# Context values computed inside an earlier attention, with two smaller edits, in a two-layer decoder kernel

## The reference, cut to what matters

```python
# layer 0, cross attention
q = _qdq(x) @ _qdq(wq).T + bq
k, v = jnp.split(cond @ wkv.T + bkv, 2, axis=-1)
attn = softmax(einsum('bnhd,bmhd->bhnm', q, k) * scale)
out = _qdq(einsum('bhnm,bmhd->bnhd', attn, v)) @ _qdq(wp).T + bp
# layer 1, cross attention
q = _rms_norm(draft_hidden @ Wq.T, q_norm_w)
kv_in = concatenate([context_hidden, draft_hidden], axis=1)
k = _rms_norm(kv_in @ Wk.T, k_norm_w)      # then rope on q and k
v = kv_in @ Wv.T                           # no norm, no rope
```

## Time and profile before

| what | value |
|---|---|
| time, median of 3 runs | 2729.94 us (2729.03 to 2731.29) |
| time of the profiled execution | 2728.3 us |
| its span | 2726.6 us, 48715 instructions |
| mean granted clock of PE | 0.951 of 2.4 GHz |
| PE, matmuls | 2479.4 us busy (91%) |
| PE, weight loads | 2033.7 us (75%) |
| DVE | 1704.5 us (63%) |
| ACT | 1154.6 us (42%) |
| POOL | 934.5 us (34%) |
| HBM | 123 GB/s over the span |

### The profile page before, as it was taken

The page is one execution under the profiler, slowest core; times in us unless marked ns, Lnnn a source line. Parts: engine busy times, 40 slices in busy tenths (PEclk is TensorE's granted clock), DMA queues, the critical chain, the costliest instruction groups (busy, mean ns, idle before and its releaser), DMA issues. The chain is left out here.

```text
span 2726.6 us, 48715 instructions
## 1 busy us (share of the span) xinstructions
PE 2479.4 (91%) x14967; PEld 2033.7 (75%) x14968; DVE 1704.5 (63%) x3211; ACT 1154.6 (42%) x2389; POOL 934.5 (34%) x943
## 2 busy tenths in 40 slices
PE   7999788879899999799997998997999998999998
PEld 7888666658688887588875886665777787888887
DVE  4536847769777666676675566866555535666564
ACT  2103256623343334455553233757655522444443
POOL 4203201134333234423333212753333312355554
PEclk9999989989899989899998988998999989999999
DMA  5544122125622055477774432444222131666664
GB/s 191 154 140 114 28 93 77 46 91 168 179 68 65 15 166 182 147 220 223 195 223 105 131 68 96 151 125 126 73 70 72 55 129 63 182 163 159 147 163 73
DMA packets 304547, 336.59 MB, mean 123 GB/s; under 512 B 149231, under 2 KB 220063, under 8 KB 302578
## 3 DMA queue, kind: packets, MB, share of 16 engines
q1 hardware_dynamic: 233170, 256.24, 30.1%
q0 software_dynamic: 20640, 51.74, 9.7%
q10 hardware_dynamic: 50560, 26.34, 3.3%
HBM read 235.70 MB, written 98.56 MB: 123 GB/s over the span
## 5 line engine op out<-in xcount | busy, mean ns | idle before, releaser
L898 PE MATMUL e_psum<-e_up_hi,hT_hi 128*128 x672 | 244.9, 365 | 14.5 <-DVE hT_lo L867 11.0
L900 PE MATMUL e_psum<-e_up_hi,hT_lo 128*128 x672 | 237.0, 353 | 0.0
L899 PE MATMUL e_psum<-e_up_lo,hT_hi 128*128 x672 | 236.4, 352 | 0.0
L1938 POOL TENSOR_TENSOR joint_a_p<-joint_a_p,joint_a_rinv 112x487 f32<-112x487 f32 x128 | 125.5, 1002 | 187.5 <-DVE joint_a_rinv L1992 187.1
L1569 POOL TENSOR_TENSOR self_a_p<-self_a_p,self_a_mx 112x448 f32<-112x448 f32 x96 | 96.1, 1002 | 205.8 <-DVE self_a_mx L1626 205.8
L898 PEld LDWEIGHTS e_psum<-e_up_hi,hT_hi 128*128 128x128 f32 x672 | 127.6, 190 | 34.7 <-issue 24.5
L794 ACT ACTIVATE e_gate<-e_psum 128x352 f32<-128x352 f32 (+1 forms) x86 | 44.5, 517 | 247.0 <-PE e_psum L900 246.6
L1997 DVE TENSOR_REDUCE joint_a_mx<-joint_psum 112x1 f32<-112x487 f32 x128 | 84.9, 663 | 101.4 <-PE joint_psum L1963 100.7
L873 DVE TENSOR_TENSOR hT_lo<-e_psum,hT_hi 128x256 fp32r<-128x256 f32 (+2 forms) x138 | 55.7, 435 | 144.8 <-ACT hT_hi L812 144.8
L1660 ACT ACTIVATE self_a_p<-self_a_p 112x448 f32<-112x448 f32 x128 | 71.6, 574 | 168.1 <-POOL self_a_p L1569 114.9
L1211 POOL TENSOR_TENSOR p_p_z<-p_p_straight,p_p_crossed 128x512 f32<-128x512 f32 x70 | 98.4, 1407 | 112.5 <-DVE p_p_crossed L1193 110.5
(11 more groups left out here) (574 smaller groups left out, 7483.0 us busy)
## 6 DMA issues: line engine op xcount, KB each, us to landing
e_up_raw<-in_L_ffn_w SPq DMA_DIRECT2D x64, 512.0 KB, 5.0
e_up_raw<-in_L_ffn_w SPq DMA_DIRECT2D x64, 352.0 KB, 4.1
e_dn_raw<-in_L_ffn_w SPq DMA_DIRECT2D x16, 1024.0 KB, 5.5
q_all<-p_p_t_stage ACTq DMA_DIRECT2D x56, 256.0 KB, 2.3
e_dn_raw<-in_L_ffn_w SPq DMA_DIRECT2D x16, 512.0 KB, 6.3
x_first<-q_all SPq DMA_DIRECT2D x32, 224.0 KB, 2.7
v_ctx<-front_c_v_stage SPq DMA_DIRECT2D x24, 250.0 KB
x_others<-k_ctx SPq DMA_DIRECT2D x8, 750.0 KB, 5.3
```

The source lines that it names most:

```text
L898: pe.matmul(out, lhs[0], rhs[0], start=k == 0, stop=False)
L899: pe.matmul(out, lhs[0], rhs[1], start=False, stop=False)
L900: return pe.matmul(out, lhs[1], rhs[0], start=False, stop=k == n_k - 1)
L1938: pool.tensor_tensor(p[:, r, 0:S], p[:, r, 0:S], rinv[:, r:r + 1].to_broadcast([T, S]), ALU.mult).then_inc(p_ready, 1)
```

## The change

It has four parts.

- **Order on ACT in the projections.** In `RopeQkvPart`, copy and store of the turned tile (L1149, L1152) come behind the square and the scaling of the step, in place of ahead of them.
- **Unread products.** In `CrossAttentionPart` the product with the identity at L1750 goes, 96 in all (three of the four heads of 32 steps), and the ring of scaled outputs has 2 buffers in place of 4.
- **Values out of the keys stage.** `ContextRopePart` has no value weight, no value products, no copies and no stores of values any more; the keys get bank 3 as a fourth.
- **Values in the first cross attention.** A new `ContextValuesPart` (`v`) makes the same 24 items there. For each SP loads a context piece of 125 tokens (lines of 500 bytes) into one buffer, ACT splits its high part, POOL its low part, PE makes 12 products in bank 7, in two halves of 6 that may stand apart in the list, DVE copies the bank, and SP stores the copy into a new DRAM tensor `v_ctx4`, from which the last projections and the joint attention now read. Bank 7 is shared with `o`: from item 9 on an item waits for the sum into x or for the split of o's turned rows, and o's turns wait for the item ahead of them (`others_in_bank`). A second `FirstWeightPart` (`fv`) loads and splits the value weight during the first three steps of `a`; `f` uses its raw buffers and starts behind it.

`beside_context_values` puts the entries into the list: `fv` twice behind each of the first three `a`; the nine first items from entry 4 of `a` on, spread over about one item a step; then two items in each batch, one that ends near the sum into x and one near the norms, with the copy and the store at an `a` entry behind.

```diff
@@ RopeQkvPart, scalar
-                i = step - LR
-                if 0 <= i < n_rot:
...
-                    act.activation(t_stage[:, i % 3, :, :], src, ACT.Copy).then_inc(t_ready, 1)
...
                     last.then_inc(z_ready, 1)
+                i = step - LR
+                if 0 <= i < n_rot:
...
+                    act.activation(t_stage[:, i % 3, :, :], src, ACT.Copy).then_inc(t_ready, 1)
...
@@ CrossAttentionPart
-        N_S, N_T, O_RING = len(s_banks), len(t_banks), 4
-        PAD = 384
+        N_S, N_T, O_RING = len(s_banks), len(t_banks), 2
...
-                    if t % W < 3:
-                        pe.matmul(ps[:, t_banks[t % N_T], PAD:512], core.ident[:, :], core.ident[:, 0:512 - PAD], start=True, stop=True)
@@ OutNormPart, tensor
                         pe.wait_ge(h_ready, m + 1)
+                        if others_in_bank:
+                            others_in_bank(pe, 2 * b + 1)
...
                         reuse(pe, ht_ready, turned)
+                        if others_in_bank:
+                            others_in_bank(pe, 2 * b)
@@ ContextRopePart
-            sp.dma_start(w_raw[:, 1, :, :], core.ins[wv]).then_inc(raw_in[1], 16)
...
-            split_weight(0)
             split_context(0)
-            split_weight(1)
...
-                for v in values_at(i):
-                    dve.wait_ge(v_mm, v + 1)
-                    reuse(dve, v_stored[v % 2], 16 * (v // 2))
-                    dve.tensor_copy(v_stage[:, v % 2, :], ps[0:CT, v_banks[v % len(v_banks)], :]).then_inc(v_ready, 1)
...
-                for m in values_at(i):
...
-                    products(pe, ps[0:CT, v_banks[m % len(v_banks)], :], lambda k: (c_hi[:, u, k, tok(n)], c_lo[:, u, k, tok(n)]),
-                             lambda k: (w_hi[:, 1, k, :], w_lo[:, 1, k, :]), KC).then_inc(v_mm, 1)
@@ ContextValuesPart, new
+        def sync(sp):
+            def load(i):
+                b, n = i // CCH, i % CCH
+                reuse(sp, c_ready, i)
+                sp.dma_start(c_raw[:, :, 0:CT], core.ins["ctxT"][b][:, :, n * CT:(n + 1) * CT]).then_inc(c_in, 16)
+            sp.wait_ge(padded, 1)
+            load(0)
+            yield
+            load(1)
+            yield
+            for i in range(n_items):
+                yield
+                yield
+                if i + 2 < n_items:
+                    load(i + 2)
+                sp.wait_ge(v_ready, i + 1)
+                sp.dma_start(v_to[i // CCH, i % CCH, 0:CT, :], v_stage[:, i % 2, :]).then_inc(v_stored[i % 2], 16)
+                yield
...
+        def scalar(act):
+            def split_high(i):
+                act.wait_ge(c_in, 16 * (i + 1))
+                reuse(act, v_mm, i - 1)
+                act.activation(c_hi[:, i % 2, :, :], c_raw[:, :, :], ACT.Copy).then_inc(c_hi_ready, 1)
...
+        def vector(dve):
...
+                dve.wait_ge(v_mm, i + 1)
+                reuse(dve, v_stored[i % 2], 16 * (i // 2))
+                dve.tensor_copy(v_stage[:, i % 2, :], ps[0:CT, bank, :]).then_inc(v_ready, 1)
...
+        def tensor(pe):
...
+                pe.wait_ge(c_ready, i + 1)
+                reuse(pe, v_ready, i)
+                bank_free(pe, i)
+                for k in range(KC):
+                    pe.matmul(out, c_hi[:, u, k, 0:CT], w_hi[:, k, :], start=(k == 0), stop=False)
+                    pe.matmul(out, c_hi[:, u, k, 0:CT], w_lo[:, k, :], start=False, stop=False)
+                    last = pe.matmul(out, c_lo[:, u, k, 0:CT], w_hi[:, k, :], start=False, stop=(k == KC - 1))
+                    if k == KC // 2 - 1:
+                        yield
+                last.then_inc(v_mm, 1)
...
@@ the order of the segment, new
+def beside_context_values(order, at_start):
...
+    for n in range(at_start):
+        first, second, third = (half, half, half + 1) if n < 2 * at_start - 14 else (half, half + 1, half + 2)
+        for h in (first, second, third):
+            at.setdefault(("a", h), []).append("v")
+        half = third
+    for b in range(B):
+        for start in (8 * b + 4,) + (8 * b + 8,) * (b + 1 < B):
+            at.setdefault(("o", start), []).append("v")
+            at.setdefault(("o", start + 1), []).append("v")
+            at.setdefault(("a", start + 18) if start + 18 <= order.count("a") - 2 else ("o", start + 1), []).append("v")
...
+        if here in (("a", 0), ("a", 1), ("a", 2)):
+            placed += ["fv", "fv"]
+        if here in (("a", 2), ("a", 3)):
+            placed += ["v"]
+        if here == ("a", 40) or name == "o" and done_o > 8 * B - 7:
+            placed += ["f"]
@@ the cross attention's segment
+                    at_start = 9
+                    fv = FirstWeightPart(g, "fv", ins["L1_xattn_Wv"], wq, wv_lo)
+                    f = FirstWeightPart(g, "f", ins["L0_ffn_wq"][0], first_hi, first_lo, behind=fv)
+                    def bank_free(pe, i):
+                        n = i - at_start
+                        if n >= 0:
+                            pe.wait_ge(o.ht_ready if n % 2 else o.added, n // 2 + 1)
-                    g.run(["landed"] + order[:90] + ["f"] + order[90:130] + [n for name in order[130:138] for n in (name, "f")] + order[138:])
+                    g.run(["landed", "fv"] + beside_context_values(attention_order(a, o, 8, 8, gap=0.95), at_start))
@@ the keys stage's segment
-                    c = ContextRopePart(g, "c", "L1_xattn_Wk", "L1_xattn_Wv", k_ctx, v_ctx, ctx_tabs, 1e-6, (0, 1, 2), (3, 4), (5, 6), last_context)
+                    c = ContextRopePart(g, "c", "L1_xattn_Wk", k_ctx, ctx_tabs, 1e-6, (0, 1, 2, 3), (5, 6), last_context)
```

More of the change, by code:

```diff
@@ L3451, in attention_order @@
     return order + extra + ["o"] * (n_o - done_o)
+def beside_context_values(order, at_start):
+    done_a, done_o, placed, at = -2, -1, [], {}
+    half = 4
+    for n in range(at_start):
[8 more added lines that the diff above has]
+            at.setdefault(("a", start + 18) if start + 18 <= order.count("a") - 2 else ("o", start + 1), []).append("v")
+    for name in order:
+        placed.append(name)
+        if name == "a":
+            done_a += 1
+            here = ("a", done_a)
+        else:
+            here = ("o", done_o)
+            done_o += 1
+        placed += at.get(here, [])
+        if here in (("a", 0), ("a", 1), ("a", 2)):
[4 more added lines that the diff above has]
+            placed += ["f"]
+    return placed
 def decoder(nc, ins, out, blocks=range(6), debug_x=None):
```

158 lines of the change are left out of this document (99 added, 59 removed).

## The result

The changed kernel takes **2742.88 us**, median of 6 runs (2740.84 to 2746.78), against 2730.61 for the kernel before in the same comparison (6 runs, 2726.08 to 2733.78): ratio **1.0049**, 95% interval 1.0037 to 1.0061. It is slower by 12 us, and the interval lies clear of 1. The forecast was 2723, faster. The profiled executions stand the same way: spans of 2741.8 and 2726.6 us, +15.2.

A forecast was written before the change was run, and what follows sets the result against it. PE was taken to bound the keys stage, ACT's order the last projections. Terms -35 - 12 + 25 + 12 + 3 = -7 us on 2728.3 gave 2721, or 2723 as a median; range 2697 to 2750.

The forecast's parts named there:

- No sign that the prediction named for being wrong: First exponential staying near 354, cross attention cycles passing 29 us, or keys stage threes staying above 17.
- Items 4 to 8, one a step: Start of the first cross attention: a step of 5.04 us becomes about 5.9, +4 after the unread products are gone.
- Item B: Second item of a cross attention cycle: +0.9 us, some 0.5 ACT's split, about 0.4 POOL; products under DVE's norms.
- The last projections: Scaling first on ACT frees PE's next turn; ring of 3.7 us becomes nearer 3.6 or 3.2: -12 us.
- The keys stage: Without values PE no longer bounds it; three items take 14.5 us in place of 19.0: -35 us, bounds -45 and -20.
- the last items, which split nothing, 6: Keys stage: the last items, which split no context, gain 6 us of the 35.
- The cross attention, start: Value weight splits +7.5, item 0 +6, items 1 to 3 +8, items 4 to 8 +4: +25 us, bounds +12 and +35.
- Steps 9 to 31: Cross attention: two items add 3.3 us to each of 5.5 cycles, 18, less 6 for the clock: +12, bounds 0 and +25.
- The tail: Cross attention's end: items 22 and 23 run where PE is free but at 1.2 GHz: +3 us, bounds 0 and +7.
- The first one: Cross attention: PE enters each cycle's last step at 1.2 GHz, 4.1 us a cycle, 23 in all: 2746 us, chance 0.27.
- The second: Items ride in PE's gaps, DVE stays the ring, cycles cost nothing; attention +20 with the tail: 2703 us, chance 0.20.
- The third: Keys stage gains only 20 us because routing and the context split are right behind PE: 2738 us, chance 0.13.

The follow-up runs named there:

- the first run: The kernel before with only the order on ACT changed (copy and store of the turned tile behind square and scaling): 2714.52 us, ratio 0.9944.
- the other repairs: Changed kernel with two raw buffers, earlier VectorE copy, later value-weight splits, output ring of one, run together with the earlier tail pieces: 2732.04 us, ratio 1.0013.
- two repairs: Changed kernel with two raw context buffers (output ring of one), or VectorE's first copies ahead of the next maxima: 2744.46 and 2746.82 us alone, 2741.42 together.

## Why the prediction was wrong, by its own steps

No sign that the prediction named for being wrong came: the first exponential is at 363.81 (361 forecast), step 2's scores at 377.17 (377), a cycle is 27.5 us (26 to 27), and the threes of the keys stage take about 15 us (14.5). What failed is the price of an item on PE, in two terms: "Items 4 to 8, one a step", +4 and measured +8.7, and "Item B adds 0.9 ... its products lie under DVE's norms", where it adds 2.0 a cycle. Two smaller terms, the last items of the keys stage and the tail, went the same way.

- **The last projections**, -12: right, -14.2, shown by the first run. Rows 7 and 8 carried it.
- **The keys stage**, -35: the mechanism was right. Plain items stand 3.6 us apart as read in the earlier trace rows; five threes (three items, one with a split) take 76.6 us where 72.5 were forecast and 98.0 were taken before. Here are ACT's squares of the kernel after, which answer to the earlier trace rows:

```profile
1112.68 0.60 ACT L2592 ACTIVATE r2c_c_square<-r2c_psum 125x512 f32<-125x512 f32 x1 [0.50 <-ACT x_last_context L2585]
1117.61 0.60 ACT L2592 ACTIVATE r2c_c_square<-r2c_psum 125x512 f32<-125x512 f32 x1 [0.50 <-ACT x_last_context L2585]
1124.13 0.60 ACT L2592 ACTIVATE r2c_c_square<-r2c_psum 125x512 f32<-125x512 f32 x1 [0.50 <-ACT x_last_context L2585]
1127.71 0.60 ACT L2592 ACTIVATE r2c_c_square<-r2c_psum 125x512 f32<-125x512 f32 x1 [0.50 <-ACT x_last_context L2585]
```

  The step that failed is "the last items, which split nothing, 6". Between the last squares the kernel before took 9.7 us and the changed one 7.7, -2: the pair from which the 3.6 us was read, 1127.04 to 1130.63, was itself among those last items, so there was nothing to gain in it. The first six gave 7.1, as forecast.
- **The cross attention, start**, +25: measured +30.6. Step 0 cost 9.1 us more (7.5 forecast). In the timeline of the kernel after the splits wait for their pieces one by one, and the first exponential comes at 363.81 against 353.94 in the earlier trace rows:

```profile
357.12 0.63 ACT L2964 ACTIVATE x_wq<-cross_fv_raw 128x512 fp32r<-128x512 f32 x1 [16.34 <-DMA cross_fv_raw<-in_L_xattn_Wv]
358.34 0.63 ACT L2964 ACTIVATE x_wq<-cross_fv_raw 128x512 fp32r<-128x512 f32 x1 [0.59 <-DMA cross_fv_raw<-in_L_xattn_Wv]
361.53 0.63 ACT L2964 ACTIVATE x_wq<-cross_fv_raw 128x512 fp32r<-128x512 f32 x1 [2.56 <-DMA cross_fv_raw<-in_L_xattn_Wv]
363.28 0.63 ACT L2964 ACTIVATE x_wq<-cross_fv_raw 128x512 fp32r<-128x512 f32 x1 [1.12 <-DMA cross_fv_raw<-in_L_xattn_Wv]
363.81 0.56 ACT L1824 ACTIVATE cross_a_p<-cross_psum,cross_a_neg 112x375 f32<-112x375 f32 x1
```

  Step 1 cost 4.2 (6 forecast), steps 2 and 3 8.6 (8). Steps 4 to 7, where "Items 4 to 8, one a step, make a step of 5.04 us (369.84 to 374.88) about 5.9: +4", took 6.7 to 7.9 us and cost 8.7: that is the term that failed. An item a step was priced as if most of its 2.8 us of products lay in PE's gaps. Against the run with the unread products alone taken out (4.6 to 5.1 us a step) it costs 2.1 us and more. Neither loads, splits nor the place of the copy is behind it: without them steps 4 to 6 take the same 6.7, 6.8 and 7.9 us, and only step 7 falls, to 6.8. That PE's own order makes these steps is argued from that; the one run with fewer products had a lower clock (steps 4 to 7 at 7.1, 5.6, 6.0 and 10.2 us) and doesn't decide it. The bound of 5 us for the landing of a context piece was wide: the median is 3.4, the longest 7.4.
- **Steps 9 to 31**, +12: measured +18.4 from step 8 on. The credit for the clock was near right: 5.75 cycles of 23.4 are 134.6 of the 139.8 us that the kernel before took, and the items hold the clock at 1.00. The price of a cycle wasn't. PE in one cycle of the kernel after, the starts of its four steps and what it waits for ahead of the items:

```profile
482.97 0.90 PE L1743 MATMUL cross_psum<-x_others 32*112 32x375 f32 x8
...
488.15 0.57 PE L2350 MATMUL cross_psum<-ident,cross_o_oq 112*128 112x112 f32 x4 [0.16 <-DVE x_last_queries L2726]
488.65 0.90 PE L1743 MATMUL cross_psum<-x_others 32*112 32x375 f32 x8
...
494.43 0.47 PE L2740 MATMUL cross_psum<-x_wq,cross_v_c_hi 128*125 128x512 f32 x1 [0.29 <-DVE x_tok L2254]
495.97 0.90 PE L1743 MATMUL cross_psum<-x_others 32*112 32x375 f32 x8
...
502.29 0.90 PE L1743 MATMUL cross_psum<-x_others 32*112 32x375 f32 x8
...
508.89 0.47 PE L2740 MATMUL cross_psum<-x_wq,cross_v_c_hi 128*125 128x512 f32 x1 [1.68 <-DVE hT_lo L2238]
510.45 0.90 PE L1743 MATMUL cross_psum<-x_others 32*112 32x375 f32 x8
```

  Steps of 5.7, 7.3, 6.3 and 8.2 us against 4.6, 5.4, 5.2 and 7.2 without items and unread products at the same clock: each grows by about 1 us, the second by 1.9, 5.0 in all where 3.8 were forecast (3.3 and the 0.5 of the unread products). In the first the turn waits for VectorE's copy of the item (488.15) and the scores stand behind it. In the last, half an item waits for the split of the turned rows (508.89), since it needs the bank that they leave, and the next scores wait behind it for the rest of its 1.5 us. Both are halves of what the prediction calls item B. For these two I had put 0.9 us together, and for the wrong engines: they cost 2.0, while ScalarE's split and GpSimd's part are 0.2 by the run without them. Item A, in the second and third steps, costs 3.0, which its 2.4 and the 0.5 of the unread products foresaw. So 1.1 us a cycle, 6.3 in 5.75 cycles, is item B, and that is the miss of this term.
- **The unread products**: "they give 0.5 where PE is the ring and nothing elsewhere" missed that they held the clock, 7.2 us in the kernel before, and they give 0.9 a cycle where the clock holds. In the changed kernel the items hold it, as the prediction's "since PE gets denser" had it, so this error took nothing from the sum.
- **The tail**, +3: measured +7.4. VectorE and SP's queue there:

```profile
617.11 0.69 DVE L2726 COPY x_last_queries<-cross_psum 125x512 f32<-125x512 f32 x1 [1.50 <-PE cross_psum L2742]
...
618.42 2.31 SPq L2955 DMA_DIRECT2D cross_fv_raw<-in_L_ffn_wq  x2
...
623.85 0.69 DVE L2971 TENSOR_TENSOR x_first_lo<-cross_fv_raw,x_first_hi 128x512 fp32r<-128x512 f32 x1 [3.50 <-ACT x_first_hi L2964]
624.46 0.75 DVE L2254 SCALAR_TENSOR_TENSOR x_tok<-cross_psum,cross_o_oqs,x_tok 112x512 f32<-112x512 f32 x1
```

  The last two pieces of the next weight are loaded from 618.42, behind a store that waits for item 22's copy (617.11 to 617.80), where they went out at 563.11 before: 33.7 us behind the last scores in place of 28.1. The low part of the first of them (623.85) stands ahead of the last sum into x on VectorE, which so began about 3 us after its products ended. The forecast counted SP's stores for the next batch's loads and forgot these. With the pieces earlier, and the other repairs, the tail was 2.1 us shorter. Another part is item 22 itself, on PE:

```profile
612.38 0.76 PE L2740 MATMUL cross_psum<-x_wq,cross_v_c_hi 128*125 128x512 f32 x1 [1.39 <-DVE hT_lo L2238]
...
617.95 0.57 PE L2350 MATMUL cross_psum<-ident,cross_o_oq 112*128 112x112 f32 x4 [0.87 <-DVE x_last_queries L2726]
```

  Its products run mostly at 1.2 GHz, and the last turn waits for its copy until 617.95, though VectorE had the turn's operand ready at 615.61: 2.3 us, near the +3 that the forecast had for the tail at that clock. About 2 us of the loss stay open.
- **The rivals.** The first one gave the time best (2746), and by luck, since its mechanism was not there: the cycles run at 1.00. The second, items in PE's gaps, is refuted by cycles of 27.5. The third had the keys stage at -20, and it gave 29. The measured time lies in the stated range, on the other side of no change.

In sum: +16.4 us of cross attention beyond the forecast, 6 of keys stage not gained, 2 gained in the last projections, and 2 in stages that nothing touches make the 22 us between -7 and +15.

## What to carry to other kernels

Work that is moved out of a full stage is worth what comes next in that stage, and costs what the order of its new stage makes of it: here 67 us of products gave back 29 us where PE was full, and cost 39 us by the profiles, 45 by the medians, against the same kernel without them, in a stage where PE looked to have gaps, since every engine there works in order and each half item stood ahead of the next scores. Price an inserted piece by what is queued behind it on its engine in every step, not by the idle share. When taking out a wait gives nothing, look for a second chain of the same length before dropping the theory: two repairs that gave nothing one by one took steps 2 and 3 from 20.4 to 18.3 us together. Look also for what the repair moved: each one alone made these steps 3 us longer, by a slower clock, a blocked instruction or a late transfer. And test the small, sure part of a change by itself: here it alone gave more than the whole.

## What the runs showed of the hardware beyond that

Products that nothing reads, 0.9 us of PE time in a cycle of 23.4, kept the granted clock at 0.92 in place of 0.77 and saved 7 us in the stage; beside real work enough for 1.00 they cost 14 (the smaller ring was in both kernels without them). VectorE's tiny op on the maxima, 0.17 us elsewhere, took 0.99 beside GpSimd's split of an item, and both ended together, at 487.08 and 487.06:

```profile
485.79 1.27 POOL L2691 TENSOR_TENSOR cross_v_c_lo<-cross_v_c_raw,cross_v_c_hi 128x504 fp32r<-128x504 f32 x1 [5.09 <-ACT cross_v_c_hi L2707]
...
486.09 0.99 DVE L1788 TENSOR_SCALAR cross_a_neg<-cross_a_mx 112x2 f32<-112x2 f32 x1
```

It happened eight times in the stage, and not once in the run with the splits left out. The rule that the prediction took from the Trainium skill (SBUF — State Buffer, Who interferes with whom) so held here too; the page gives it for VectorE instructions that use both of its port pairs, which a tensor_scalar can do. The 17 us that the prediction worked out from it did not come. Of the two splits in a cycle only one stood full beside such an op, and with 22 of the 24 splits left out a cycle is 0.2 us shorter. In the cycle shown the only wait that the trace has for PE between 485.66 and the next scores at 488.65 is 0.16 us, for VectorE's copy: PE's order, not the maxima, ended the step.
